# x turned to token-major by VectorE and sixteen transfers instead of by PE, the first handover reordered, the normalisations in halves

## What is computed

```python
x = x + xattn(layernorm(x), ctx)          # 32 heads over 2048 + 128 keys
x = x + mamba(layernorm(x))
x = x + ffn(layernorm(x))                 # 1792 wide, one of every 32 kept

# mamba, 128 heads of 64 channels, 8 groups, one chunk of 128 tokens:
proj = h @ in_proj_w.T                    # gate 8192 | x 8192, B, C 1024 each | dt 128
x, B, C = silu(causal_conv4(...))
dt = softplus(dt + dt_bias)
M = (C @ B.T) * exp(segment sums of A*dt)     # per head, lower triangle
y = M @ (x * dt) + D * x
out = (y * rsqrt(mean(y^2)) * norm_w * silu(gate)) @ out_proj_w.T
```

## Time and profile before

| | us |
|---|---|
| median of 3 runs (range) | 623.66 (622.91 to 623.95) |
| profiled execution, its own time | 624.35 |
| its span, first to last instruction | 622.6 |
| PE busy in the span | 604.3 (97%) |
| DVE, ACT, POOL busy | 414.1, 349.4, 308.9 |
| PE idle before the segments (L1871) in the mamba and later stages | 6.6, in two places |

### The profile page before, as it was taken

How to read it: one execution, slowest core, us unless ns; L and a number is a source line. 1 busy time by engine, 2 the same in 40 slices (tenths; PEclk the granted TensorE clock), 3 DMA queues, 4 the chain that set the end, 5 groups by cost and what they waited for, 6 DMA issues and landing times.

```text
span 622.6 us, 11085 instructions
## 1 busy us (share of the span) xinstructions
PE 604.3 (97%) x3934; PEld 532.9 (86%) x3934; DVE 414.1 (67%) x875; ACT 349.4 (56%) x617; POOL 308.9 (50%) x212
## 2 busy tenths in 40 slices
PE   8999999999999999999999989996999999999997
PEld 7888888899998889899988989995989989898573
DVE  5433047678888888888886668694473764748773
ACT  4303125577776867686766535566657566567110
POOL 0000011369778877887786612239786486571000
PEclk9999999999999999999999999997999999999999
DMA  8301021878887788778769929472767758798500
GB/s 344 145 0 35 1 66 35 215 192 212 214 213 200 202 212 212 200 200 217 178 168 247 343 109 301 161 306 104 267 216 284 274 195 321 254 365 336 193 1 17
DMA packets 29694, 120.68 MB, mean 194 GB/s; under 512 B 7712, under 2 KB 8224, under 8 KB 22096
## 3 DMA queue, kind: packets, MB, share of 16 engines
q1 hardware_dynamic: 28912, 118.96, 60.8%
q10 hardware_dynamic: 576, 1.05, 0.5%
q0 software_dynamic: 160, 0.07, 0.1%
HBM read 86.30 MB, written 0.26 MB: 139 GB/s over the span
## 4 chain that ended last, share of the span: by engine, by line
PE 77%; DVE 6%; POOL 6%; ACT 5%; issue 4%; DMA 1%; DVEq 0%; ACTq 0%; SPq 0%; POOLq 0%
PE ps L1857 19%; PE ps L1561 12%; PE ps L1563 12%; PE ps L1562 12%; PE ps L1659 4%; POOL pt_lo L574 3%; PE ps L1892 3%; PE ps L1903 2%; PE ps L1735 2%; PE ps L2040 2%; PE ps L1602 2%; DVE prob_far L1209 2%; PE ps L1619 2%; POOL v_lo L574 2%; PE ps L2003 2%
## 5 line engine op out<-in xcount | busy, mean ns | idle before, releaser
L574 POOL TENSOR_TENSOR pt_lo<-far_t,pt_hi 128x512 fp32r<-128x512 f32 (+1 forms) x94 | 112.1, 1218 | 54.6 <-ACT pt_hi L722 54.5
L1857 PEld LDWEIGHTS ps<-norm_t,ring 128*128 128x128 f32 x1152 | 131.8, 192 | 2.6 <-issue 1.4
L1857 PE MATMUL ps<-norm_t,ring 128*128 128x128 f32 x1152 | 133.4, 276 | 0.0
L796 ACT ACTIVATE prob_far<-prob_far,neg_max 128x1024 f32<-128x1024 f32 (+2 forms) x96 | 85.5, 892 | 54.9 <-DVE neg_max L1213 54.9
L1209 DVE TENSOR_SCALAR_CACHE_REDUCE prob_far<-ps 128x256 f32<-128x256 f32 (+2 forms) x96 | 86.8, 906 | 31.9 <-PE ps L1563 31.5
L1390 DVE SCALAR_TENSOR_TENSOR acc<-ps,cw,acc 128x127 f32<-128x127 f32 (+2 forms) x240 | 63.3, 340 | 18.8 <-ACT acc L969 18.7
L1233 DVE STREAM_TRANSPOSE prob_far<-prob_far 128x2176 f32<-128x2176 f32 x30 | 73.1, 2437 | 0.8 <-ACT prob_far L796 0.2
L574 POOL TENSOR_TENSOR v_lo<-v_all,v_hi 128x256 fp32r<-128x256 f32 (+2 forms) x12 | 16.6, 1389 | 104.2 <-ACT v_hi L722 104.2
L1561 PE MATMUL ps<-pt_hi,v_hi 128*128 128x256 f32 x208 | 61.2, 294 | 2.8 <-POOL pt_lo L574 2.4
L1561 PE MATMUL ps<-k_hi,q_hi 128*128 128x512 f32 (+2 forms) x160 | 61.4, 384 | 1.4 <-ACT v_all L722 0.7
L969 ACT ACTIVATE acc<-ps,cb,cw 128x128 f32<-128x128 f32 x80 | 30.1, 457 | 52.0 <-PE ps L1857 52.0
(11 more groups left out here) (255 smaller groups left out, 1267.1 us busy)
## 6 DMA issues: line engine op xcount, KB each, us to landing
ring<-w_in_dram SPq DMA_DIRECT2D x36, 1024.0 KB, 4.9
far_t<-prob_far SPq DMA_DIRECT2D x240, 136.0 KB, 2.6
ring<-w_out_dram SPq DMA_DIRECT2D x16, 1024.0 KB, 4.9
ring<-wq_dram SPq DMA_DIRECT2D x16, 512.0 KB, 4.0
ring<-wo_dram SPq DMA_DIRECT2D x16, 512.0 KB, 3.7
w_sb<-w_dram SPq DMA_DIRECT2D x4, 896.0 KB, 9.1
ring<-ctx_t_dram SPq DMA_DIRECT2D x3, 1024.0 KB, 4.9
ring<-w_dram SPq DMA_DIRECT2D x3, 1024.0 KB, 8.8
```

The lines of the kernel that those rows point to most:

```text
L574: sub = lambda dst, a, hi: pool.tensor_tensor(dst, a, hi, ALU.subtract)
L796: nc.scalar.activation(tile, tile, ACT.Exp, bias=neg_max[:, b, h:h + 1], accum_out=part_sum[:, b, h, i:i + 1]).then_inc(exp_ok, 1)
L1857: ins = mm(ps[:, bank, t * T:t * T + T], w[:, t, c, :], norm_t[:, c, :], start=(c == 0), stop=(c == NC - 1))
```

## The change

x is no longer transposed by PE, except for group 0. `turn_x(g)` on DVE transposes blocks of 32 by 32 of the group's x into the two `acc` buffers taken as one tile of 128x1024; SP then issues sixteen transfers of 32 partitions by 1 KB (`x_moves`), which put the blocks in their places in the new tile `x_tok`. `x_times_dt` reads `x_tok` and a copy of the step sizes that is kept in PSUM bank 7, in two instructions, for even and odd heads. Since `acc` holds the turned x until the transfers have landed, ACT waits for them before the next `first_tap`. `turn_x(g+1)` stands at the end of step g on DVE, behind `gate(g)`. On SP `x_moves(g)` stands behind `in_load(g, 1)` and `out_load(g-1, 1)` and ahead of `in_load(g, 2)`. `y_product` takes over the waits of `x_transposes`.

Around group 0 the order changes on ACT, POOL and SP: the output weights of group 0 are loaded ahead of `in_load(1, 0)` and rounded earlier, `decay_exp(2)` comes ahead of the rounding of the gated result, and the rounding of `c2` moves behind step 4. The second and third normalisation take epsilon inside the square root and do the scaled rows, the transposes and the copy to `norm_t` in two halves, in two banks.

The diff, cut to its core:

```diff
@@ buffers
-                sbuf(st4, "at_end", [P, HPG, HALF_T])
+                x_tok = sbuf(st4, "x_tok", [P, 4, TPG, 32])
-                acc = [sbuf(st4, f"acc{b}", [P, 4, T]) for b in range(2)]
+                acc_all = sbuf(st4, "acc", [P, 2, 4, T])
+                acc = [acc_all[:, b, :, :] for b in range(2)]
+                x_turn = acc_all[:].rearrange("p b c t -> p (b c t)").rearrange("p (j t k) -> p j t k", j=4, k=32)
@@ block.sync
-            with sp.Fori(0, 3) as turn:
-                for i in range(2):
-                    g = turn * 2 + (i + 1)
-                    in_load(g, 0)
-                    in_load(g, 1)
-                    out_load(turn * 2 + i, 0)
-                    out_load(turn * 2 + i, 1)
-                    in_load(g, 2)
-                    in_load(g, 3)
+            def x_moves(g):
+                sp.wait_ge(x_turned, g)
+                sp.wait_ge(xdt_ok, g)
+                for i in range(4):
+                    for j in range(4):
+                        sp.dma_start(x_tok[32 * j:32 * j + 32, i, :, :],
+                                     x_turn[32 * i:32 * i + 32, j, :, :]).then_inc(x_there, 16)
+
+            out_load(0, 0)
+            out_load(0, 1)
+            in_load(1, 0)
+            in_load(1, 1)
+            x_moves(1)
+            in_load(1, 2)
+            in_load(1, 3)
+            with sp.Fori(2, GROUPS - 1) as g:
+                in_load(g, 0)
+                in_load(g, 1)
+                out_load(g - 1, 0)
+                out_load(g - 1, 1)
+                x_moves(g)
+                in_load(g, 2)
+                in_load(g, 3)
             for c in range(NC):
                 sp.dma_start(w1_sb[:, c, :], w1[c]).then_inc(w1_in, 16)
             for g in (GROUPS - 2, GROUPS - 1):
                 for i in range(2):
                     out_load(g, i)
+            x_moves(GROUPS - 1)
@@ block.gpsimd
+            pool.memset(eps_c[:], EPS).then_inc(ident_ok, 1)
+                if g == 0:
+                    pool.wait_ge(m_ok, 2)
+                    out_low(0, 0)
@@ block.scalar
             def norm_sqrt(k):
-                act.wait_ge(ln, LN_STEPS * k + 3)
-                nc.scalar.activation(rstd[:, 1:2], rstd[:, 0:1], ACT.Sqrt).then_inc(ln, 1)
+                act.wait_ge(ln, LN_STEPS * k + 2)
+                nc.scalar.activation(rstd[:, 1:2], mean_var[:, 1:2], ACT.Sqrt, bias=eps_c[:]).then_inc(ln, 1)
+                for half in range(2):
+                    act.wait_ge(ln_turn, 2 * k + half + 1)
+                    copy(norm_t[:, 2 * half:2 * half + 2, :],
+                         ps[:, 6 + half, 0:2 * P].rearrange("p (c t) -> p c t", c=2)).then_inc(ln_ev, 1)
...
             decay_exp(0, 0, 1)
+            act.wait_ge(gm_ps, 1)
+            out_high(0, 0)
             first_tap(step_chunk(0, 1), 7, 1, 12, 1)
...
             squares(0)
-            act.wait_ge(gm_ps, 1)
-            out_high(0, 0)
-            u_high(0)
-            act.wait_ge(ysq_ok, 1)
-            out_high(0, 1)
-            act.wait_ge(stack_in, 96)
-            copy(c2_st[:], c2_sb[:]).then_inc(c2h_ok, 1)
...
-            def mamba_step(g, b, last=False):
+            def mamba_step(g, b, last=False, handover=False):
                 k, o = 2 * g + 6, 1 - b
                 decay_exp(g + 1, o, 0)
+                if handover:
+                    u_high(0)
+                    act.wait_ge(ysq_ok, 1)
+                    out_high(0, 1)
+                act.wait_ge(x_there, MOVED * g)
                 first_tap(step_chunk(g, 0), k, 0, 8 * g + 8, 0)
...
                 if last:
+                    act.wait_ge(xdt_ok, GROUPS)
+                    w1_split(2)
                     w1_split(3)
@@ block.vector, norm(k)
-                nc.vector.tensor_scalar(rstd[:, 0:1], mean_var[:, 1:2], EPS, None, ALU.add).then_inc(ln, 1)
-                nc.vector.tensor_scalar(normed[:], res[:], mean_var[:, 0:1], rstd[:, 2:3],
-                                        ALU.subtract, ALU.mult).then_inc(ln, 1)
+                for half in range(2):
+                    cols = slice(half * 2 * P, (half + 1) * 2 * P)
+                    nc.vector.tensor_scalar(normed[:, cols], res[:, cols], mean_var[:, 0:1], rstd[:, 2:3],
+                                            ALU.subtract, ALU.mult).then_inc(ln, 1)
@@ block.vector, mamba
+            def turn_x(g, b):
+                dve.wait_ge(silu_ok, 2 * g + 6)
+                nc.vector.transpose(x_turn.rearrange("p j t k -> p t j k"),
+                                    xc[b][:].rearrange("p t (j k) -> p t j k", k=32)).then_inc(x_turned, 1)
             def x_times_dt(g):
-                dve.wait_ge(xt_ps, g + 1)
-                nc.vector.tensor_tensor(xdt[:], ps[:, 4:6, :].rearrange("p a (h c) -> p (a h) c", c=64),
-                                        dt[:, bass.ds(g * HPG, HPG)].unsqueeze(2).to_broadcast([P, HPG, 64]),
-                                        ALU.mult).then_inc(xdt_ok, 1)
+                dve.wait_ge(x_there, MOVED * g)
+                dve.wait_ge(dt_home, 1)
+                for odd in range(2):
+                    heads = ps[:, 7, bass.ds(g * HPG, HPG)].rearrange("p (t o) -> p o t", o=2)[:, odd, :]
+                    ins = nc.vector.tensor_tensor(
+                        xdt[:].rearrange("p (t o) (i c) -> p o i t c", o=2, c=32)[:, odd, :, :, :],
+                        x_tok[:, 2 * odd:2 * odd + 2, :, :],
+                        heads.unsqueeze(1).unsqueeze(3).to_broadcast([P, 2, TPG, 32]), ALU.mult)
+                ins.then_inc(xdt_ok, 1)
...
+            dve.wait_ge(gm_ok, 1)
+            nc.vector.tensor_copy(ps[:, 7, 0:NH], dt[:]).then_inc(dt_home, 1)
...
             taps_of(7, 1, 12, 1)
             skip_add(0, 0)
+            turn_x(1, 1)
             mask_decay(1, 1, 0)
             mask_decay(1, 1, 1)
             gate(0, 0)
...
                 mask_decay(g + 1, o, 1)
                 taps_of(k + 1, 1, 8 * g + 12, 1)
                 gate(g, b)
+                turn_x(g + 1, o)
@@ block.tensor
-            def x_transposes(g, b):
+            def first_x_transposes():
...
             def y_product(g, b):
                 pe.wait_ge(xdt_ok, g + 1)
+                if isinstance(g, int) and g == 1:
+                    pe.wait_ge(y_ok, 1)
+                elif not (isinstance(g, int) and g == 0):
+                    pe.wait_ge(ug_ok, 2 * g)
...
             def mamba_step(g, before_g, b, first):
-                x_transposes(g, b)
                 segments(g + 1, 1 - b, 0)
...
-            x_transposes(7, 1)
             out_proj(6, ug, 0)
             y_product(7, 1)
```

More of the change, by code:

```diff
@@ L81 @@
 STACK = 80
-LN_STEPS = 8
+LN_STEPS = 6
 WARM = 12
@@ L773, in _ @@
             k_split(0, 1)
[L774 to L775 removed]
+            norm_evac(0)
+            act.wait_ge(ln_ev, 2)
             copy(lat_hi[:], norm_t[:]).then_inc(c_hi, 1)
@@ L1075, in mamba_step @@
                 gate_out(step_chunk(g, 2), 0, sg[o][:, 0:4, :])
-                if last:
-                    w1_split(2)
-                else:
+                if not last:
                     out_high(g, 1)
@@ L1081, in mamba_step @@
                 if last:
+                    act.wait_ge(xdt_ok, GROUPS)
+                    w1_split(2)
                     w1_split(3)
-            with act.Fori(0, 2) as turn:
+            mamba_step(1, 1, handover=True)
+            mamba_step(2, 0)
+            with act.Fori(1, 2) as turn:
                 for i in range(2):
                     mamba_step(turn * 2 + (i + 1), 1 - i)
+            act.wait_ge(stack_in, 96)
+            copy(c2_st[:], c2_sb[:]).then_inc(c2h_ok, 1)
             mamba_step(5, 1)
@@ L1095, in _ @@
             norm_sqrt(2)
-            norm_evac(2, 7)
-            copy(norm_hi[:], ps[:, 7, :].rearrange("p (c t) -> p c t", c=NC)).then_inc(nh_ok, 1)
+            norm_evac(2)
+            copy(norm_hi[:].rearrange("p (b c) t -> p b (c t)", b=2), ps[:, 6:8, 0:2 * P]).then_inc(nh_ok, 1)
             act.wait_ge(r1_ps, 1)
-            copy(r1_st[:], ps[0:STACK, 6, 0:T]).then_inc(r1h_ok, 1)
+            copy(r1_st[:], ps[0:STACK, 5, 0:T]).then_inc(r1h_ok, 1)
             for i in range(4):
@@ L1448, in _ @@
                 taps_of(k, k % 2, tile, FIRST_BANK[m])
-            x_times_dt(0)
+            first_x_times_dt()
             dve.wait_ge(gm_ps, 1)
@@ L1551, in _, with norm_transpose @@
             mm = nc.tensor.matmul
-            def norm_transpose(k, bank):
-                pe.wait_ge(ln, LN_STEPS * k + 6)
-                for c in range(NC):
-                    ins = nc.tensor.transpose(ps[:, bank, c * P:c * P + P], normed[:, c * P:c * P + P], ident[:])
-                ins.then_inc(ln, 1)
+            def norm_transpose(k, places):
+                for half, (bank, at) in enumerate(places):
+                    pe.wait_ge(ln, LN_STEPS * k + 5 + half)
+                    for i in range(2):
+                        c = 2 * half + i
```

(20 more changed lines are left out.)

53 lines of the change are left out of this document (31 added, 22 removed).

## The result

The kernel after takes 662.82 us (median of 4 runs, 662.32 to 663.96) beside 623.42 us (622.91 to 623.95) of the kernel before on the same chip: a ratio of 1.0634, with a 95% interval of 1.0616 to 1.0653. It is slower by 39.4 us. The prediction said 672, and 650 to 686. The profiled execution took 663.96 us, with a span of 662.2.

A forecast was written before the change was run, and what follows sets the result against it. PE was taken to bound the kernel, with one dent behind group 0. Span 622.6 + 2.7 (first M) + 44.8 (loops) + 2.7 (slow start, last group) - 1.7 (normalisations) = 671.1; time 672 us, range 650 to 686.

The forecast's parts named there:

- The mechanism: Mamba steps: DVE's turn, sixteen SP issues, landing, x times dt and mask hold up PE, in steps of 32 us.
- M: Moment the second half of `segments` starts on PE: 428.65 for step 1, 479.69 for step 3, before the change.
- Loops: From first M to `y_product(7)`: five loops of 32.3 us plus 31.1, 192.8 against 148.0, so 44.8 more.
- The clock stays up: Rival: full PE clock despite idling in the steps, loops of 30.4 us, time 658; chance 0.15, in some or all steps.
- First M: Handover behind group 0: M moves from 428.65 to 431.4, 2.7 us later, waiting for the first transfers.
- The two masks and the gate lie inside that wait: First handover on DVE: both masks (2.4 us) and gate (2.2) fit between the turn at 416.8 and transfers at 428.8.
- Normalisations: Second and third normalisation in halves: 0.85 us saved each, 1.7 for two.
- The gaps are under 0.5: Sign to look for after the change: PE's waits in the normalisations under 0.5 us; before, 0.56 and 0.69.
- PE's idle time in a loop: Each mamba step: PE idles 6.2 us ahead of M, with the clock down behind it.
- the other side: Rival: x arrives before anybody waits, first M at 424.0, 4.7 us earlier, 2.7 of slow clock gone, time 612; chance 0.05.

The follow-up runs named there:

- eight_moves: Kernel after with eight of the sixteen transfers a group, x times dt reading the first half twice: 624.66 us, ratio 1.002 against the kernel before.
- two_queues: Kernel after with the same sixteen transfers, eight issued by SP and eight by ACT: 645.17 us, ratio 1.0349 against the kernel before.
- quarter_bytes: Kernel after with all sixteen transfers but rows of 256 bytes, three quarters of x zero: 662.41 us, ratio 1.0616 against the kernel before.
- warm_filler: Kernel after with 20 unread identity matmuls on PE ahead of the second half of `segments`: 655.74 us, ratio 1.051 against the kernel before.
- mask_first: Kernel after with DVE's mask ahead of x times dt, for groups from 2 on: 655.44 us, ratio 1.0511 against the kernel before.
- norms_alone: Kernel before with only the halved normalisations added: 622.45 us, ratio 0.9981 against the kernel before.
- no_turn: Kernel after with x transposed by PE again, reordered handover and halved normalisations kept: 619.58 us, ratio 0.9939 against the kernel before.
- mask_then_gate: no_turn with x times dt (1) and group 2's first mask ahead of group 0's gate on DVE: 617.39 us, ratio 0.99 against the kernel before.

## Why the prediction was right

**The mechanism, right in each link.** Turn, sixteen issues, landing, x times dt, mask, M: the rows of DVE and SP after show them in this order with nothing between. ACT's first tap and the weight loads behind the moves cost nothing, as foretold: DVE's taps follow the mask without a wait (461.18), and PE never waits for a weight load in these steps. eight_moves and two_queues show that it is the count of issues in one queue, and quarter_bytes that it is not the bytes.

**The terms.** Measured in the profiled spans, 622.6 to 662.2, the 39.6 us come from three places: the first M is 0.3 later (428.94 against 428.65 in the earlier trace rows); from it to `y_product(7)` are 185.8 us against 148.0, 37.8 more; and from `y_product(7)` to the end 47.4 against 45.9, 1.5 more. The prediction had 2.7, 44.8 and 2.7, less 1.7. Its misses in the first two places, 2.4 and 7.0 us, have the same sign, and the third is 0.5 the other way, so the 662.8 lie 9 below the 672 and hardly any luck of opposite errors is in it.

- *Loops: 192.8 predicted, 185.8 measured.* This is the term that was mis-sized, in two parts of it. The moves were there 12.1, 11.4, 11.8, 11.5 and 11.5 us after the turn and not 12.0, since 32 KB land in 1.8 us and not in the 2.4 taken from larger ones (the first of these five took 12.1 all the same, because SP needed 10.82 us for its sixteen); with the last group that is some 2.4 us less. The gate ended 16.6 us after M in the first step, as predicted, but 15.6 to 16.1 in the five that follow, where 16.6 was carried through: in sum 4.1 us. The price of an issue (0.59), the turn (1.24, of which 1.15 behind the gate) and the mask with its handoff were right; x times dt with the mask is 2.47 from start to M against 2.58, another 0.7 in six places.
- *The clock stays up: a rival at 658.* The time alone would not decide against it: 662.8 lies nearer to 658 than to 672. The windows do: the clock was down behind every one of the seven idle stretches (0.50 to 0.55 in some 3 us). From the second loop on it came back sooner than in the earlier trace rows: 0.69 already from 464 to 467. This fits the shorter way from M to the gate there, and in warm_filler, with the clock up, that way is 13.8 us in the first two loops. That is less than the prediction's 14.7 for full clock, and its loop of 30.4 is 28.8 to 30.0 there, so the rival was too dear as well; why is open. The filler recovers 7 us in all.
- *First M: 431.4 predicted, 428.94 measured.* The chain was as told, turn at 413.86, transfers there at 426.47, M. It started 1.8 earlier than in the kernel before. 0.6 of that is the second normalisation, which the prediction counts in another term; the attention layer ended 1.2 us earlier in this profile (359.68 against 360.91 for the first matmul of L1899 and its counterpart). With the same code up to there, eight_moves starts it at 360.15 and mask_first at 360.69, so these starts differ between runs by up to 1.0 us; what moves them is open, and that part of the miss is chance. "The two masks and the gate lie inside that wait" held, and the wait covered more than was known: the masks took 2.87 us and the gate 4.28 instead of 2.4 and 2.2, and PE idled another 2.47 us for the masks at 417.96, all of it ahead of the transfers' landing.
- *Normalisations: 0.85 each predicted.* The second one went from 1.25 us of gaps to 0.58, thus 0.7; both together 1.1 us in norms_alone, against 1.7. The gaps are under 0.5, as foretold.
- *PE's idle time in a loop: 6.2 predicted, 5.2 to 5.9 measured* (4.85 at the first M), which is the shorter loop over again. The clock averages 0.961.

**The second queue.** The Trainium skill, "DMA: Bandwidth & Descriptors", section "Issuing engines are not separate DMA queues", says that a second initiating engine only saves the sequencer's time. two_queues agrees: SP's 10.8 us become 5.6, and nothing else in the chain becomes shorter. That this time is usually small relative to the DMA does not hold here, with 10 us of issuing ahead of a landing of 1.8.

**What went wrong behind the prediction.** no_turn was expected at 613, from the prediction's own working of the other side: 4.7 us at the first M and 2.7 of clock. The clock's share came (it averages 1.00 in that span), and step 2 starts at 444.39 instead of 450.42; but M came at 425.22, with PE idle 1.18 and 1.95 us on the way to it. The two masks and the gate of group 0, 2.35 and 2.18 us in the kernel before, took 3.65 and 4.29. The durations came from a moment when POOL stood still beside the masks and came second beside the gate. mask_then_gate takes away the second of these waits; measured against the kernel before of its own chip it gains 5.6 us where no_turn gains 4.0. The steps 2 to 6 also took 123.1 us (444.39 to 567.48) instead of 121.8 (450.42 to 572.25). The rest of the missing 6 us is open.

## What to carry to other kernels

Count the issues of a transfer pattern before its bytes: a turn cut into blocks of 32 partitions cost 0.6 us an issue here, one behind the other in one queue, and it must fit between the last reader of the old data and the first reader of the new. A wait at the head of an engine's step delays all that is queued behind it, but moving it back only uncovers the next reader: the chain itself has to become shorter or start earlier. When work is pulled forward, look at what POOL does at that moment, since DVE's durations there are not those of a quiet stretch.

## What the runs showed of the hardware

**DVE and POOL hold each other up on SBUF.** The gate's line in the kernel before and after, by operands (count, then minimum, median and maximum in ns):

```profile
L1431 DVE SCALAR_TENSOR_TENSOR ug<-yv_sb,nw,sg x8: 343/343/345, 417.8 to 419.7; 128x128 f32<-128x128 f32 x8
```

```profile
L1482 DVE SCALAR_TENSOR_TENSOR ug<-yv_sb,nw,sg x8: 339/339/2443, 417.8 to 421.8; 128x128 f32<-128x128 f32 x8
```

DVE and POOL at that time, in the kernel before and then in the kernel after:

```profile
415.56 2.35 DVE L1409 TENSOR_TENSOR decay<-decay,gm 128x1024 f32<-128x1024 f32 x2
417.83 2.18 DVE L1431 SCALAR_TENSOR_TENSOR ug<-yv_sb,nw,sg 128x128 f32<-128x128 f32 x8
...
418.88 3.38 POOL L681 TENSOR_TENSOR sq_sum<-sq_sum,ysq 128x1024 f32<-128x1024 f32 x1 [3.92 <-ACT ysq L994]
```

```profile
417.83 4.28 DVE L1482 SCALAR_TENSOR_TENSOR ug<-yv_sb,nw,sg 128x128 f32<-128x128 f32 x8
...
417.14 2.98 POOL L701 TENSOR_TENSOR sq_sum<-sq_sum,ysq 128x1024 f32<-128x1024 f32 x1 [1.45 <-ACT ysq L1025]
...
427.67 1.22 DVE L1444 TENSOR_TENSOR decay<-ps,gm 128x1024 f32<-128x1024 f32 x1
...
425.59 2.35 POOL L594 TENSOR_TENSOR ring_lo<-ring,out_hi1a 128x1024 fp32r<-128x1024 f32 x1
```

One of eight equal instructions takes 2443 ns instead of 339. In the kernel after, POOL adds its squares, SBUF to SBUF, until 420.12; the gate's first instruction starts at 417.83 and ends at 420.27, just behind it. In the kernel before the gate had begun first: it took 2.18 us, and POOL's sum 3.38 instead of the 2.40 of the later steps. In no_turn the building of `at_lo` on POOL takes 2.12 us in place of 1.15 and a mask beside it 2.15 in place of 1.22, so it goes both ways. With its first operand in PSUM a mask takes its 1.22 us beside POOL's work on the low part of the weights, which takes its 2.35 too (last two rows). The gate with its first operand in PSUM is never over 352 ns either, but POOL's sum of squares is over by then (443.37 against 443.42), so that shows nothing. The Trainium skill, "SBUF — State Buffer", section "Who interferes with whom", has the rule: a DVE instruction with two inputs in SBUF contends with a GpSimd instruction that reads SBUF, and the one that comes second blocks until the first is through. The trace agrees, in the durations, in who came second, and in the mask's PSUM form, which is spared.

**The clock fell behind idle stretches of about 2 us, but not behind all of them.** The kernel after has a short one of its own, ahead of the first half of `segments(2)`; it lies inside the wait for the first transfers and costs nothing. Below stand PE's row and the window behind it, and the window behind 1.98 us idle in warm_filler:

```profile
417.96 0.74 PE L1929 MATMUL ps<-at_pair,pair_r 128*128 128x512 f32 x1 [2.47 <-DVE decay L1444]
```

```profile
417.96:420.90 2.94, 2.94 (x11) 2.65 (x12) 2.94 (x4) 1.41 (x2) 2.16 (x1) 0.52 0.18 50
```

```profile
518.82:521.80 2.98, 2.98 (x17) 2.24 (x19) 2.98 (x12) 1.01 (x1) 1.31 (x2) 0.51 1.03 432
```

The granted clock averages 0.52 and 0.51, and in eight_moves 0.75 behind 1.72 us idle (523.60 to 526.00). It stayed at 1.00 behind 1.95 us idle in no_turn (425.20 to 428.20) and behind 2.15 in two_queues (481.80 to 484.80). So the length of the last idle stretch alone does not tell; what else decides was not tried.

**An issue has a price of its own.** 0.59 us in the median for 32 partitions, with rows of 256 bytes, of 1 KB, and with the 136 KB of the earlier trace rows, where 1 MB over 128 partitions is issued in 0.33. Whether the partitions or the pattern make the difference was not tried, and neither was the same move in fewer transfers over more partitions.
